# Graph network with mixtures, one core: TensorE loops in the first mixture, attention's terms one unit sooner

## The reference, cut to what matters

```python
def _L0_ffn_ref(x, router_w, router_b, w1, b1, w2, b2):
    probs = jax.nn.softmax(jnp.einsum('bsd,de->bse', x, router_w) + router_b, axis=-1)
    top_p, top_i = jax.lax.top_k(probs, 2)
    ...
    for e in range(8):
        h = jax.nn.gelu(jnp.einsum('bsd,df->bsf', x, w1[e]) + b1[e], approximate=False)
        y = jnp.einsum('bsf,fd->bsd', h, w2[e]) + b2[e]
        out = out + combine[..., e:e + 1] * y
```

```python
    e = jax.nn.leaky_relu(a_src[src] + a_dst[dst], 0.2)
    m = jax.ops.segment_max(e, dst, num_segments=n)
    ex = jnp.exp(e - m[dst])
    alpha = ex / (segment_sum(ex, dst)[dst] + EPS)
    out = segment_sum(alpha[:, :, None] * h[src], dst)
```

## Time and profile before

| | |
|---|---|
| three runs | 3143.19, 3144.93, 3146.76 us; median 3144.93 |
| the profiled execution | 3143.14 us, its span 3141.3 us |
| mean granted TensorE clock | 0.909 |
| TensorE busy | 2654.7 us (85%) in 13285 matmuls |
| VectorE busy | 2125.4 us (68%) |
| ScalarE busy | 1305.6 us (42%) |
| chain of waits, largest lines | L815 15%, L905 10%, L1152 8%, L952 7%, L1049 6% |

### The profile page before, as it was taken

One profiled execution on the slowest core, in us unless ns is written; L12 is line 12 of the kernel. 1 busy time (PEld: TensorE's weight loads), 2 busy tenths in 40 slices (PEclk: granted clock), 3 DMA queues, 4 the chain that ended last, 5 costly groups with the idle time before them and its releaser, 6 DMA issues.

```text
span 3141.3 us, 42158 instructions
## 1 busy us (share of the span) xinstructions
PE 2654.7 (85%) x13285; PEld 2161.0 (69%) x13285; DVE 2125.4 (68%) x4317; ACT 1305.6 (42%) x2600; POOL 725.1 (23%) x902
## 2 busy tenths in 40 slices
PE   5979999697999756789998999588968888987998
PEld 2536666484799734779898999547635545676998
DVE  7978888885676565898777777657673346764322
ACT  0036666571477521666555566317221103352110
POOL 4858888600266511000000000200010000000000
PEclk8989999898999875999999999788988799976999
DMA  9700110160142304776665466510001000002210
GB/s 314 234 29 30 30 37 30 47 183 30 35 49 49 31 16 143 259 249 215 205 208 203 170 237 221 187 41 1 29 36 54 23 17 29 17 1 91 82 69 24
DMA packets 72665, 310.33 MB, mean 99 GB/s; under 512 B 22857, under 2 KB 23294, under 8 KB 67259
## 3 DMA queue, kind: packets, MB, share of 16 engines
q1 hardware_dynamic: 51616, 272.78, 27.8%
q0 software_dynamic: 20816, 34.51, 3.5%
HBM read 260.52 MB, written 46.70 MB: 98 GB/s over the span
## 4 chain that ended last, share of the span: by engine, by line
PE 66%; DVE 17%; POOL 5%; issue 5%; DMA 3%; ACT 3%; SPq 1%; POOLq 0%; DVEq 0%; ACTq 0%
PE PS L815 15%; PE PS L905 10%; PE PS L1152 8%; PE PS L952 7%; PE PS L1049 6%; PE PS L1051 3%; POOL logits L708 2%; PE PS L938 2%; DVE w1s L2131 2%; PE PS L1070 2%; PE PS L1072 2%; PE PS L1071 2%; PE PS L1133 1%; DVE w2s L2136 1%; POOL F L696 1%
## 5 line engine op out<-in xcount | busy, mean ns | idle before, releaser
L815 PE MATMUL PS<-large_rows,turned 125*128 x1448 | 527.6, 367 | 39.1 <-issue 18.4
L815 PE MATMUL PS<-small_rows,turned 125*128 x1448 | 492.1, 343 | 0.0
L708 POOL DMA_INDIRECT logits<-lgr,key x362 | 362.5, 1001 | 245.8 <-DVE lgr L1772 175.8
L1049 PE MATMUL PS<-urowsT,w1s 128*128 128x384 f32 (+2 forms) x1164 | 366.4, 378 | 57.3 <-issue 33.1
L905 PE MATMUL PS<-WB,XT 128*125 128x384 f32 (+1 forms) x1120 | 387.7, 506 | 0.0
L815 PEld LDWEIGHTS PS<-large_rows,turned 125*128 125x128 f32 x1448 | 272.6, 188 | 87.4 <-issue 75.2
L905 PEld LDWEIGHTS PS<-WB,XT 128*125 128x125 f32 x1120 | 212.2, 192 | 159.8 <-issue 34.7
L952 PE MATMUL PS<-F,PT 125*125 125x96 f32 (+3 forms) x1500 | 294.0, 349 | 19.2 <-ACT PT L1358 8.2
L1051 PE MATMUL PS<-urowsT,w1s 128*128 128x192 f32 (+2 forms) x1164 | 303.4, 261 | 7.2 <-issue 7.2
L1049 PEld LDWEIGHTS PS<-urowsT,w1s 128*128 128x128 f32 x1164 | 229.4, 197 | 89.6 <-issue 63.4
L815 PEld LDWEIGHTS PS<-small_rows,turned 125*128 125x128 f32 x1448 | 272.3, 188 | 8.1
(11 more groups left out here) (345 smaller groups left out, 4944.0 us busy)
## 6 DMA issues: line engine op xcount, KB each, us to landing
XN<-in_L_ffn_w SPq DMA_DIRECT2D x98, 769.0 KB, 4.3
PB<-in_L_ffn_w SPq DMA_DIRECT2D x97, 768.0 KB, 5.5
WB<-node_ids SPq DMA_DIRECT2D x44, 512.0 KB
logits<-NEG SPq DMA_DIRECT2D x8, 1367.2 KB
WB<-logits SPq DMA_DIRECT2D x5, 2187.5 KB
slot_rows<-NEG POOLq DMA_DIRECT2D x13, 768.0 KB, 57.4
slot_outs<-NEG POOLq DMA_DIRECT2D x12, 768.0 KB, 93.6
C<-in_L_ffn_expert_w SPq DMA_DIRECT2D x8, 1152.0 KB, 5.3
```

The costliest lines, as they stand in the source:

```text
L708: pool.indirect_dma_start(out=table, out_offset=bass.IndirectOffsetOnAxis(ap=key[:, i:i + 1], axis=0), in_=lgr[:, i % EU, 0:HEADS[g]["h"]] ...
L815: mm = pe.matmul(out, ohT[i % 3][:, (1 - side) * P:(2 - side) * P], part[side][:, bass.ds(c, 1), a:b].rearrange("p o n -> p (o n)"), start ...
L1049: pe.matmul(both(q % 2, columns), w1s[:, g % 2, 0, w:w + P], urowsT2[:, :, k * TU:k * TU + columns], start=k == 0, stop=False)
```

## The change

On TensorE, in the first mixture: the nested Ifs become one loop over 12 units with one If in it; the 12 groups of each variant become a loop of five passes over two groups, and two groups written out. Buffer parities and banks now come from k and c (0 or 1); the values waited for are computed from registers. `second` no longer opens a sum. Instead `clear` does four matmuls of one row with start set into banks 2 to 5, behind a wait for s_uy that has moved from `second` of group 0 to the end of the previous unit, behind `first` of the next unit's group 0. In attention: ScalarE makes the terms of unit s + 1 ahead of the exponential of s - 1, and TensorE's spreading of the next head stands before the head's fourth unit instead of its fifth.

```diff
--- before.py
+++ after.py
@@ -964,7 +964,7 @@
                     pe.wait_ge(s_ast, gats + 1)
                     broadcast(0)
                 for s in range(units):
-                    if kind == "gat" and place(s)[1] == T - 1 and place(s)[0] + 1 < h:
+                    if kind == "gat" and place(s)[1] == T - 2 and place(s)[0] + 1 < h:
                         broadcast(place(s)[0] + 1)
                     turn(s)
                     if s:
@@ -1024,8 +1024,8 @@
 
                     if b == 0:
                         pe.wait_ge(s_ux, u * 16 + 16)
-                    if b == 2:
-                        wait(pe, s_ha, u * (NG * FC) - 1)
+                    if b == 2 and not isinstance(u, int):
+                        pe.wait_ge(s_ha, u * (NG * FC) - 1)
                     for k in range(2):
                         for s in range(SU):
                             tr = pe.transpose(PS[:, TURN[b], k * TU + s * P:k * TU + (s + 1) * P],
@@ -1036,60 +1036,69 @@
 
                     return PS[:, bank, :].rearrange("p (j n) -> p j n", j=2)[:, :, 0:columns]
 
-                def first(u, g, columns=TU):
-
-                    pe.wait_ge(s_lo1, u * NG + g + 1)
-                    if g == 0:
-                        pe.wait_ge(s_ul, u * (KD // 2) + KD // 2)
+                def first(done, k, columns=TU, fresh=None):
+
+                    pe.wait_ge(s_lo1, done + (k + 1))
+                    if fresh is not None:
+                        pe.wait_ge(s_ul, fresh)
                     for c in range(FC):
-                        q = g * FC + c
-                        wait(pe, s_ha, u * (NG * FC) + q - 1)
-                        for k in range(KD):
-                            w = (k * FC + c) * P
-                            pe.matmul(both(q % 2, columns), w1s[:, g % 2, 0, w:w + P],
-                                      urowsT2[:, :, k * TU:k * TU + columns], start=k == 0, stop=False)
-                            mm = pe.matmul(PS[:, q % 2, 0:columns], w1s[:, g % 2, 1, w:w + P],
-                                           urowsT2[:, 0, k * TU:k * TU + columns], start=False, stop=k == KD - 1)
+                        for kk in range(KD):
+                            if kk == 0:
+                                wait(pe, s_ha, done * FC + (k * FC + c - 1))
+                            w = (kk * FC + c) * P
+                            pe.matmul(both(c, columns), w1s[:, k % 2, 0, w:w + P],
+                                      urowsT2[:, :, kk * TU:kk * TU + columns], start=kk == 0, stop=False)
+                            mm = pe.matmul(PS[:, c, 0:columns], w1s[:, k % 2, 1, w:w + P],
+                                           urowsT2[:, 0, kk * TU:kk * TU + columns], start=False, stop=kk == KD - 1)
                         mm.then_inc(s_ua, 1)
 
-                def second(u, g, columns):
-
-                    pe.wait_ge(s_lo2, u * NG + g + 1)
-                    if g == 0:
-                        wait(pe, s_uy, u)
+                def second(done, k, columns, closes=False):
+
+                    pe.wait_ge(s_lo2, done + (k + 1))
                     for c in range(FC):
-                        pe.wait_ge(s_hl, (u * NG + g) * FC + c + 1)
-                        opens, closes = g == 0 and c == 0, g == NG - 1 and c == FC - 1
-                        large = [hid2[:, g % 2, c, 0:P], hid2[:, g % 2, c, 192:192 + P]]
-                        small = [hid2[:, g % 2, c, 320 + P * s:320 + P * (s + 1)] for s in range(2)]
-                        pair = hid2[:, g % 2, c, P:2 * P]
+                        pe.wait_ge(s_hl, done * FC + (k * FC + c + 1))
+                        ends = closes and c == FC - 1
+                        large = [hid2[:, k % 2, c, 0:P], hid2[:, k % 2, c, 192:192 + P]]
+                        small = [hid2[:, k % 2, c, 320 + P * s:320 + P * (s + 1)] for s in range(2)]
+                        pair = hid2[:, k % 2, c, P:2 * P]
                         for half in range(2):
                             w = c * D + half * 384
-                            w_large, w_small = w2s[:, g % 2, 0, w:w + 384], w2s[:, g % 2, 1, w:w + 384]
+                            w_large, w_small = w2s[:, k % 2, 0, w:w + 384], w2s[:, k % 2, 1, w:w + 384]
                             out = PS[:, 2 + half, 0:384]
-                            pe.matmul(out, large[0], w_large, start=opens, stop=False)
-                            pe.matmul(out, large[0], w_small, start=False, stop=False)
-                            mm = pe.matmul(out, small[0], w_large, start=False, stop=closes)
+                            pe.matmul(out, large[0], w_large, start=False, stop=False, skip_group_check=True)
+                            pe.matmul(out, large[0], w_small, start=False, stop=False, skip_group_check=True)
+                            mm = pe.matmul(out, small[0], w_large, start=False, stop=ends, skip_group_check=True)
...
                     mm.then_inc(s_ub, 1)
 
+                def clear():
+
+                    for bank in range(2, 6):
+                        pe.matmul(PS[:, bank, 0:384], ones[0:1, 0:P // 2].bitcast(BF16),
+                                  ident[0:1, 1:2].bitcast(BF16)[:, 0:1].to_broadcast([1, 384]), start=True, stop=False,
+                                  skip_group_check=True)
+
                 def groups(u, columns):
 
-                    for g in range(NG - 1):
-                        first(u, g + 1, columns)
-                        if g == NG - 2:
-                            turn(u + 1, 0)
-                            turn(u + 1, 1)
-                        second(u, g, columns)
+                    with pe.Fori(0, NG // 2 - 1) as p:
+                        done = u * NG + p * 2
+                        for k in range(2):
+                            first(done, k + 1, columns)
+                            second(done, k, columns)
+                    done = u * NG + (NG - 2)
+                    first(done, 1, columns)
+                    turn(u + 1, 0)
+                    turn(u + 1, 1)
+                    second(done, 0, columns)
                     turn(u + 1, 2)
-                    second(u, NG - 1, columns)
+                    second(done, 1, columns, closes=True)
 
                 def unit(u):
 
@@ -1103,22 +1112,19 @@
                             groups(u, 3 * TU // 4)
                     with pe.Else():
                         groups(u, TU)
-                    first(u + 1, 0)
+                    first(u * NG + NG, 0, fresh=u * (KD // 2) + KD)
+                    pe.wait_ge(s_uy, u + 1)
+                    clear()
 
                 pe.wait_ge(s_plan, 3)
                 units = pe.value_load(nunits[0:1, 0:1], min_val=1, max_val=NU)
                 for b in range(KD // 2):
                     turn(0, b)
-                first(0, 0)
-                unit(0)
-
-                def units_from(u):
+                first(0, 0, fresh=KD // 2)
+                clear()
+                with pe.Fori(0, NU) as u:
                     with pe.If(units > u):
                         unit(u)
-                        if u + 1 < NU:
-                            units_from(u + 1)
-
-                units_from(1)
 
             def mixture1():
                 w1 = WB[:, 0:3456].rearrange("p (e k f) -> p e k f", e=6, k=KD)
@@ -1338,13 +1344,18 @@
                     act.wait_ge(s_astp, gats + 1)
                     act.copy(AT[0:h], PSz[0:h, 0:T * P].rearrange("h (t n) -> h t n", t=T)[:, :, 0:R])\
                        .then_inc(s_ast, 1)
+                def terms(s):
+                    head, t = place(s)
+                    act.wait_ge(s_bc, heads + head + 1)
+                    wait(act, s_tp, every + s - 3)
+                    act.activation(W[0:R, s % 4, :], PSz[0:R, 0:N], ACT.Identity, scale=-1.0,
+                                   bias=a_d[:, t, head:head + 1]).then_inc(s_v, 1)
+
+                if kind == "gat":
+                    terms(0)
                 for s in range(units + 2):
-                    if kind == "gat" and s < units:
-                        head, t = place(s)
-                        act.wait_ge(s_bc, heads + head + 1)
-                        wait(act, s_tp, every + s - 3)
-                        act.activation(W[0:R, s % 4, :], PSz[0:R, 0:N], ACT.Identity, scale=-1.0,
-                                       bias=a_d[:, t, head:head + 1]).then_inc(s_v, 1)
+                    if kind == "gat" and s + 1 < units:
+                        terms(s + 1)
                     if kind != "average" and 1 <= s <= units:
                         v = s - 1
                         act.wait_ge(s_lm, soft + v + 1)
```

More of the change, by code:

```diff
@@ L1072, in second @@
-                            mm = pe.matmul(out, small[0], w_large, start=False, stop=closes)
+                            pe.matmul(out, large[0], w_large, start=False, stop=False, skip_group_check=True)
+                            pe.matmul(out, large[0], w_small, start=False, stop=False, skip_group_check=True)
```

(7 more changed lines are left out.)

4 lines of the change are left out of this document (2 added, 2 removed).

## The result

The kernel with the change takes **3098.32 us** (median of four runs, 3094.10 to 3099.70), the kernel before on the same chip 3144.06 us (3141.20 to 3146.76): ratio 0.9852, 95% interval 0.9835 to 0.9869. The profiled execution took 3099.70 us, its span 3097.9. The forecast was 3101 us, and "faster" with a chance of 0.71. So the number was hit, but two of its terms were off in opposite directions and cancelled: the first mixture gained less than was forecast, and attention gained where a small loss was forecast.

The account below looks back on a forecast made before the run. TensorE was taken to bound the first mixture, except two VectorE-bound units. Pauses 42.4, less 9 for clearing and waits, plus 15 clock, less 3 first exit, give 45 us; attention costs 1.5; net 43.5 gives 3101 us, range 3088 to 3186.

Parts of the forecast that it names:

- The bound and the pauses: First mixture: units are TensorE's except the first two, VectorE's; TensorE's 42.4 us of pauses at seven unit changes go.
- One sign: First mixture: TensorE's granted clock (PEclk) stays near 1.0 at changes of unit from the second on.
- I take the good end: First mixture's outer loop: jumps in some 1,250 instructions cost nothing; at worst 4.3 to 6.2 us each.
- A: Rival, first mixture: outer loop's jumps fetch code again, up to 6.2 us at seven changes; about 3186 us, chance 0.24.
- The first narrow exit, 3 us: First mixture: the first exit from the narrow variant leads to never-fetched code and still costs 3 us.
- Register waits at nothing: First mixture: six waits per group with values from registers instead of constants cost nothing.
- C: Rival, first mixture: register waits slow every group, +29 us against the gain of 45; about 3130 us, chance 0.05.
- Clearing and head of unit: First mixture's unit changes: four clearing matmuls cost 0.7 us, the unit's head 0.1 more; 9 us in all with waits.
- The slow clock, 15 us: First mixture: the lower clock after pauses goes; of 41 us a quarter is idle, the rest gains 15 us.
- Attention, +1.5: Attention stages: pause per head stays 2.7 us; third terms ahead of the first exponential add 1.5 us, bounds -3 and +4.
- D: Rival, attention: the spreading's pause shrinks by half at 14 head changes, 19 us more gain; about 3082 us, chance 0.03.

Follow-up runs that it names:

- group_loops_only: Kernel after the change, loops over groups kept but the twelve units written out one behind the other as before: 3148.59 us, ratio 0.9988 against before.
- the size series: Kernel after the change with more groups written out in some or all variants, outer loop 1,093 to 3,222 instructions: ratios to before from 0.9842 to 1.0051.
- after: The kernel with the whole change, against the kernel before; outer loop of 1,093 instructions: 3098.32 us, ratio 0.9852.
- eight_in_full: Kernel after the change with eight groups instead of four written out in the full variant alone, loop of 1,493 instructions: ratio 0.9842 against before.
- late_clear: Kernel after the change, clearing moved behind the jump, load and branches, waiting for s_ha instead of s_uy: 3092.89 us, ratio 0.9818 against before.
- both_further: Kernel after the change with the next head's spreading one more unit ahead: 3067.92 us, ratio 0.9750 against before.
- spread_only: Kernel after the change with ScalarE's terms in the old order, spreading still one unit sooner: 3070.82 us, ratio 0.9759 against before.
- att_only: Kernel before with the change's attention part alone: 3139.99 us, ratio 0.9972 against before.

## Why the prediction was right, and where it wasn't

1. **The bound and the pauses: right.** Of the 42.4 us of pauses, 40.1 were "issue", TensorE's own code, and a loop that is kept removes them: 6.6 us of issue are left (forecast below 12), 7 packets (below 15). (The other 2.3 us were waits for w1s, of which 0.8 stay.) group_loops_only and the size series show the cause, not only the effect: the pauses come back with the code alone, at the same arithmetic. One sign was not met: the clock was to stay near 1.0 from the second change on, and it fell for 3.4 us at the second and the last.
2. **"I take the good end": right, by less than it looked.** 1,093 instructions are kept and so are 1,493, but 1,861 are not wholly. With twelve groups written out A would have won, at +16 us. Nothing in the trace of before could give the room, so that the good end came true is in part luck, and the forecast's 0.24 for A says so. The Trainium skill, in Runtime: NRT & Kernel Launch, section Instruction fetch mechanics, gives a store of 2,048 instructions; the runs show that the room for an outer loop with forward jumps is smaller, under 1,861. Its rule that a taken branch out of a window of two pages forces a fetch is not borne out by after and eight_in_full: the jump back there crosses four to six packets and fetches nothing.
3. **The first narrow exit, 3 us: right in kind**, measured 3.98.
4. **Register waits at nothing: right.** VectorE's sums return every 6.01 us in narrow units, as in the earlier trace rows, and full groups still take 8.32 us. C is out.
5. **Clearing and head of unit: mechanism right, one size off.** The clearing takes the 0.7 us that were forecast (0.82 from 1603.15 to the modelled end of its last matmul). "The head of the unit 0.1 more" is 0.5 to 1.3 us at the fourth to the seventh change: a jump back, a load and branches stand behind a wait here, so that TensorE's sequencer has not done them ahead. In late_clear the same instructions stand ahead of the wait, and no idle time is left behind the clearing.
6. **The slow clock, 15 us: over-sized.** TensorE's busy time says 10. Of the time at the lower level 34.2 us went; 10 times 2 were work, so some two fifths of it was idle, where a quarter was taken. Idle time fell by 32.8 us where the steps give some 35: the first narrow exit has 1.0 more, and the waits and heads of units some 1.7 (5.8 for 4.1). The clearings cost 5.6 for 4.9, eight in place of seven. Together that is the way from 45 to 37 us.
7. **Attention, +1.5: wrong in sign.** "The pause per head stays 2.7 us" is right to 0.03 us in the 8-head stage (with four heads it is 3.6 to 4.4 us before and 3.7 to 5.0 after), and both_further and spread_only show the reason given, that the two edits cancel. The sum then took from an unchanged pause that the time is unchanged. But the granted clock around those pauses did change: with the new order it fell at one change of head in the last stage where it had fallen at three, -7.3 us there, and -9 in all (att_only). No bound of the forecast had room for it, and why the clock does so stays open. Against the measured times the forecast has attention some 10 us too slow and the mixture 8 us too fast, and that is why 3101 came out: the nearness of the number is luck.
8. **D: right that the pause doesn't shrink, but half the change does shrink it**: to 0.65 us, with -28 us. The "reason that I do not see" was there: it wasn't asked what each edit does without the other.

Two slips of the forecast change nothing. There are 13 changes of head (7, 3 and 3) and not 14. And the chances of "faster" add up to 0.72.

## What to carry to other kernels

Where one engine's straight code is what bounds a stage ("issue" pauses behind jumps, packets of instructions in them), loop over all of it, and count what one pass of the outer loop contains, skipped variants included: on this kernel some 1,500 instructions are kept, at 1,861 some 10 of the mixture's 37 us of gain are left, and from 2,165 on the loop is slower than the straight code was. When a change moves both the producer and the consumer of a wait by one step, weigh each alone: here the spreading alone brought some 28 us more than both together, and both together only 9. And put what a unit must wait for behind its branches and loads, not ahead of them.

## What the runs showed of the hardware that was not expected

- A loop that is too long is worse than straight code: with 2,165 or 3,222 instructions a change of unit pauses up to 13.1 us where the longest pause at a change in the straight code is 3.9 to 6.2 us, and mixture and total are some 20 and 16 us longer.
- Between 2,165 and 3,222 instructions the length makes no difference, and at 1,861 only the jumps from a full unit back to a three-quarter one pause (12.36 and 9.97 us). Which packets are given up, and in what order, these runs do not show.
- A different order of ScalarE's work, with TensorE's pauses of the same length, changed the granted clock of the last attention stage from 0.77 to 0.88; the stage takes 71.1 us in both kernels with the old order and 63.8 in all eight with the new. It stays open why.
